# A mixer and mixture-of-experts layer on one core: row normalisation of the last mixer block on ScalarE, and four smaller moves

## What is computed

```python
xn = layernorm(x)                       # no gamma, no beta
# mixer
xi, g = split(xn @ W_in.T)              # 512 -> 2 x 1024
u  = silu(causal_conv4(xi) + conv_b)
h_t = 0.95 * h_(t-1) + 0.05 * (u_t @ W_B.T)     # 64 states, per sequence
y  = (h @ W_C.T + D_param * u) * silu(g)
mixer = layernorm(y @ W_out.T + xn) * ln_gamma + ln_beta
# experts, 8 of them; each takes its 1024 best rows
scores = (tanh(xn @ gate_w.T) + 1) / 2
vals, idx = top_k(scores.T, 1024)
r = layernorm(xn[idx]) * ffn_gamma + ffn_beta
o = (gelu(r @ fc1.T + b1) @ fc2.T + b2) * vals
out = x + mixer + scatter_add(xn, idx, o)
```

## Time and profile before

| | us |
|---|---|
| three runs | 2670.35, 2671.75, 2673.03 |
| median | 2671.75 |
| profiled execution, its own time | 2671.86 |
| its span, first to last instruction | 2670.1 |
| PE, DVE, ACT, POOL busy | 2633.7, 2057.1, 1490.4, 674.4 |
| mean granted TensorE clock | 0.998 of full |

### The profile page before, as it was taken

One profiled execution on the slowest core, in us unless ns is written; L12 is line 12 of the kernel. 1 busy time (PEld: TensorE's weight loads), 2 busy tenths in 40 slices (PEclk: granted clock), 3 DMA queues, 4 the chain that ended last, 5 costly groups with the idle time before them and its releaser, 6 DMA issues.

```text
span 2670.1 us, 41531 instructions
## 1 busy us (share of the span) xinstructions
PE 2633.7 (99%) x11818; PEld 2135.5 (80%) x11820; DVE 2057.1 (77%) x3533; ACT 1490.4 (56%) x2570; POOL 674.4 (25%) x1002
## 2 busy tenths in 40 slices
PE   8999999999999999999999999999999999999998
PEld 3588888888887788888788888888888888888886
DVE  8778888887887788888876777867778677786654
ACT  5744555555555565665445555565555655556553
POOL 5422222222222122223422213213132131321102
PEclk9999999999999999999999999999999999999999
DMA  9733222223333322235444425334253342533313
GB/s 364 259 126 111 81 92 89 91 93 104 111 111 111 110 73 87 87 93 160 142 131 109 124 64 137 90 92 133 64 136 90 91 132 65 136 90 89 99 54 71
DMA packets 139517, 299.99 MB, mean 112 GB/s; under 512 B 26080, under 2 KB 26208, under 8 KB 135520
## 3 DMA queue, kind: packets, MB, share of 16 engines
q1 hardware_dynamic: 105696, 201.54, 23.0%
q0 software_dynamic: 33664, 96.75, 14.7%
HBM read 244.46 MB, written 53.77 MB: 112 GB/s over the span
## 4 chain that ended last, share of the span: by engine, by line
PE 94%; DVE 2%; issue 1%; ACT 1%; DMA 1%; POOL 0%; SPq 0%; DVEq 0%; ACTq 0%; POOLq 0%
PE po L2485 9%; PE ring L1546 9%; PE po L2487 9%; PE po L2486 9%; PE ring L1547 8%; PE ring L1548 8%; PE pb L2485 4%; PE pb L2487 4%; PE pb L2486 4%; PE po L1584 4%; PE po L1585 4%; PE po L1586 4%; PE pc L2487 2%; PE pc L2485 2%; PE pc L2486 2%
## 5 line engine op out<-in xcount | busy, mean ns | idle before, releaser
L2485 PE MATMUL po<-w2h,hid_h 128*128 128x512 f32 x1024 | 402.2, 393 | 1.1 <-DVE hid_l L2422 1.0
L1546 PE MATMUL ring<-xt_h,w_h 128*128 128x512 f32 x1024 | 400.1, 391 | 0.1
L2486 PE MATMUL po<-w2l,hid_h 128*128 128x512 f32 x1024 | 398.6, 389 | 0.0
L1547 PE MATMUL ring<-xt_l,w_h 128*128 128x512 f32 x1024 | 398.5, 389 | 0.0
L1548 PE MATMUL ring<-xt_h,w_l 128*128 128x512 f32 x1024 | 398.4, 389 | 0.0
L1339 DVE SCALAR_TENSOR_TENSOR u<-xin,cw,u 128x512 f32<-128x512 f32 x384 | 288.4, 751 | 74.3 <-issue 32.8
L1967 POOL DMA_INDIRECT out_dram<-res,idx_c x64 | 108.6, 1697 | 476.7 <-DVE res L2332 464.7
L1546 PEld LDWEIGHTS ring<-xt_h,w_h 128*128 128x128 f32 x1024 | 192.3, 188 | 40.9 <-DVE xt_l L542 0.9
L2485 PEld LDWEIGHTS po<-w2h,hid_h 128*128 128x128 f32 x1024 | 192.3, 188 | 40.9 <-DVE hid_l L2422 1.4
L1548 PEld LDWEIGHTS ring<-xt_h,w_l 128*128 128x128 f32 x1024 | 192.2, 188 | 40.1
L1547 PEld LDWEIGHTS ring<-xt_l,w_h 128*128 128x128 f32 x1024 | 192.3, 188 | 39.3
(11 more groups left out here) (296 smaller groups left out, 6306.2 us busy)
## 6 DMA issues: line engine op xcount, KB each, us to landing
w2r<-fc_in SPq DMA_DIRECT2D x256, 256.0 KB
wo<-wo_halves POOLq DMA_DIRECT2D x120, 512.0 KB, 4.2
w1r<-fc_in SPq DMA_DIRECT2D x144, 256.0 KB
x_tail<-x_in SPq DMA_DIRECT2D x64, 256.0 KB, 2.8
out_dram<-res SPq DMA_DIRECT2D x64, 256.0 KB, 2.0
g_x<-x_in SPq DMA_DIRECT2D x15, 1024.0 KB, 8.4
xt_rows<-g_xnt SPq DMA_DIRECT2D x15, 1024.0 KB, 10.1
rows<-xt_rows SPq DMA_DIRECT2D x15, 1024.0 KB, 6.2
```

The source lines that it names most:

```text
L1546: pe.matmul(ring[r % 2][:, :], w_h[:, r, q], xt_h[:, k, :], start=(k == 0), stop=False)
L1547: pe.matmul(ring[r % 2][:, :], w_h[:, r, q], xt_l[:, k, :], start=False, stop=False)
L2485: pe.matmul(dst, ah, bh, start=start, stop=False, skip_group_check=more)
L2486: pe.matmul(dst, ah, bl, start=False, stop=False, skip_group_check=more)
```

## The change

It has five parts.

1. In the last block the first 512 rows are normalised without gamma and beta, by ACT (`normal_row`), two tiles ahead of the last gate eviction and two behind the cast of group 2. POOL adds `-mean * rstd` per tile for it. Gamma and beta come in when the transposed rows are evicted: there they are per-partition columns (`f_ln_c`, a new small load). `group_high` evicts with scale and bias into `yt_whole`, and then casts. The last `group_high` stands ahead of `first_high` and `normal_rows`. `t_low` reads `yt_whole`. DVE's `normalise` for this group is gone.
2. POOL issues `load_wo` for groups 4 and 5 ahead of and between the gate gathers.
3. In the first two one-hot blocks the fifth one-hot goes from behind group 4 to behind group 3 (`HOT_AT`); `PLACE_AT` stays.
4. The three casts of small weights in the gate stage go into the last group, one in each of its first three blocks, ahead of the wait for the scores.
5. At the start SP sets 37 semaphores ahead of the gate weights and of the second load of x. In the first expert pass the third and fourth row tile of expert 1 move from steps 13 and 14 to 12 and 13.

```diff
@@ stage_gate, sync
+        m.counts.start(sp, sums.counts)
+        m.counts.start(sp, m.counts.counts[begun:own])
         sp.dma_start(gw[:, :, :], t["gate_w"]).then_inc(c_gw, 16)
         load_x(1, 1)
-        m.counts.start(sp, sums.counts)
-        m.counts.start(sp, m.counts.counts[begun:own])
@@ stage_gate, scalar
+        def small_high(i):
+            if i == 0:
+                act.wait_ge(c_win, 48 + 1)
+                act.copy(w.wc_hh[:, :], staged2[:, 0:2, :].rearrange("p a b -> p (a b)")).then_inc(c_sh, 1)
...
         def group(h, first=False, last=False):
...
                     normalise(b + 1, (i + 1) % R)
+                if last and i < 3:
+                    small_high(i)
                 act.wait_ge(c_se, (b + 1) * KD + 1)
@@ Experts
         self.yt_end = m.ends_at["xt_l"]
+        self.yt_w = m.over("yt_whole", self.yt_end, KD * TB * 4, [P, KD, TB])
...
-    def inverse_std(self, pool, g, half):
+    def inverse_std(self, pool, g, half, with_shift=False):
...
+            if with_shift:
+                pool.wait_ge(self.c_rs, n + 1 + 1)
+                pool.tensor_scalar(self.std[:, j:j + 1], self.mv[:, j, 0:1], self.rstd[:, j:j + 1], -1.0, ALU.mult,
+                                   ALU.mult).then_inc(self.c_g, 1)
+
+    def normal_row(self, act, j):
+        act.wait_ge(self.c_g, j + 1 + 1)
+        act.activation(self.rows[:, j, :], self.rows[:, j, :], ACT.Identity, bias=self.std[:, j:j + 1],
+                       scale=self.rstd[:, j:j + 1]).then_inc(self.c_nm, 1)
@@
-HOT_AT = 2 * ((START, 0, 1, 2, 4, 5),) + 4 * ((START, 0, 1, 3, 5),)
+HOT_AT = 2 * ((START, 0, 1, 2, 3, 5),) + 4 * ((START, 0, 1, 3, 5),)
@@ stage_mixer, sync
+        sp.dma_start(ew.columns[:, :, :], t["f_ln_c"]).then_inc(ew.c_small, 16)
@@ stage_mixer, gpsimd, turn
             if last:
-                ew.inverse_std(pool, 0, ends.half)
+                ew.inverse_std(pool, 0, ends.half, True)
                 for j in range(J):
+                    if j % 2 == 0:
+                        load_wo(b, WO + j // 2)
                     ew.gather_gates(pool, 0, j)
                 ends.twice_scale(pool, b)
-            for c in range(WO, NC_):
+            for c in range(WO + 2 if last else WO, NC_):
                 load_wo(b, c)
@@ stage_mixer, scalar
         def group_high(k):
             act.wait_ge(c_t, k + 1 + 1)
-            act.copy(xt_h[:, k, :], rows_out[k % 2][:, :]).then_inc(c_th, 1)
+            if k == 0:
+                act.wait_ge(ew.c_small, 16 + 1)
+                act.wait_ge(c_ag, NB * NW + 1)
+            act.activation(ew.yt_w[:, k, :], rows_out[k % 2][:, :], ACT.Identity, bias=ew.columns[:, 1, k:k + 1],
+                           scale=ew.columns[:, 0, k:k + 1]).then_inc(c_whole, 1)
+            act.wait_ge(c_whole, k + 1 + 1)
+            act.copy(xt_h[:, k, :], ew.yt_w[:, k, :]).then_inc(c_th, 1)
...
             if last:
+                ew.normal_row(act, 0)
+                ew.normal_row(act, 1)
                 in_g(b, 7)
             y_high(b, 2)
+            if last:
+                ew.normal_row(act, 2)
+                ew.normal_row(act, 3)
...
+                if last and k == KD - 1:
+                    group_high(k)
                 if last and k >= 2:
                     sums.first_high(act, k - 2)
                 ends.normal_rows(act, b, k)
-            if last:
-                group_high(KD - 1)
@@ stage_mixer, vector
         def t_low(n, k, last=False):
             dve.wait_ge(c_th, n + 1 + 1)
-            dve.tensor_tensor(xt_l[:, k, :], rows_out[k % 2][:, :] if last else next_x[:, k * TB:(k + 1) * TB],
+            dve.tensor_tensor(xt_l[:, k, :], ew.yt_w[:, k, :] if last else next_x[:, k * TB:(k + 1) * TB],
...
         def expert_rows(c):
...
-            if 1 <= c < 1 + J:
-                ew.normalise(dve, 0, c - 1, rows)
             if c == J:
                 ew.keep(dve, 0, 0)
@@ stage_experts
-    TAIL_AT, ROWS_1_AT, ROWS_2_AT = (4, 5, 6, 7), (3, 5, 7, 8), (9, 11, 13, 14)
+    TAIL_AT, ROWS_1_AT, ROWS_2_AT = (4, 5, 6, 7), (3, 5, 7, 8), (9, 11, 12, 13)
```

More of the change, by code:

```diff
@@ L591, in normalise @@
                                scale=rstd[i % 2][:, j:j + 1]).then_inc(c_xa, 1)
+        def small_high(i):
+            if i == 0:
+                act.wait_ge(c_win, 48 + 1)
+                act.copy(w.wc_hh[:, :], staged2[:, 0:2, :].rearrange("p a b -> p (a b)")).then_inc(c_sh, 1)
+            elif i == 1:
+                act.copy(w.wc_lh[S:P, :], staged2[S:P, 0:2, :].rearrange("p a b -> p (a b)")).then_inc(c_sh, 1)
+            else:
+                act.wait_ge(c_id, 4 + 1)
+                act.copy(w.wb[:, :, 0:S], staged2[:, 3, :].rearrange("p (c s) -> p c s", s=S)).then_inc(c_sh, 1)
         def group(h, first=False, last=False):
@@ L639, in __init__ @@
         self.rstd = m.sb("f_rstd", [P, J])
+        self.columns = m.sb("f_columns", [P, 2, KD])
         self.c_w1 = [m.count(f"f_w1_{i}") for i in range(4)]
```

15 lines of the change are left out of this document (6 added, 9 removed).

## The result

The changed kernel takes **2662.45 us** (median; 2662.04 to 2663.16) against 2671.78 us for the kernel before, measured beside it. The ratio is 0.9965, with a 95% interval from 0.9955 to 0.9976: 9.3 us, or 0.35%, less. One of the seven runs of the changed kernel took 5414.03 us in a slow state and is left out of the lowest-to-highest times and of the ratio. The profiled execution of the changed kernel took 2662.32 us, its span is 2660.6 us; before it was 2671.86 and 2670.1.

The account below looks back on a forecast made before the run. PE was taken as busy for 99% of the span, so only its own waits could pay. The terms -3.9 - 1.2 - 0.7 - 1.1 + 0 made -6.9 us against 2671.86, giving 2665.0 us, range 2662.6 to 2668.3.

Parts of the forecast that it names:

- The last block, -3.9: Last mixer block: normalising off DVE starts the experts at 1305.5 against 1309.38; -3.9 us, ends 0 and -5.9.
- The estimate from the Trainium skill's formula: Last block's gate gather: 2.0 us plus bytes at 436 GB/s lands it at 1290.6; share 5 loses nothing, 0.6 more gained.
- The one-hots, -1.2: First two one-hot blocks: moving the fifth one-hot gives -0.6 us each, -1.2 in all; ends +0.8 and -1.5 each.
- The expert row work, -1.1: First expert pass: earlier row work removes PE's wait for a low half and its restart; -1.1 us, ends +0.5 and -1.1.
- The casts, -0.7: Gate stage, 13th block: moving three ACT casts removes PE's wait for normalised rows; -0.7 us, ends 0 and -0.7.
- the next floor: Gate stage: DVE's statistics, released by a load, come next and limit the gain from the casts to -0.7 us.
- The start, 0: SP's semaphore increments ahead of gate weights and second x load: no gain or loss; 0, ends -0.3 and +2.1 us.
- Rival 1: Last block: gate gathers land behind the second weight load, share 5 starts 2.2 us later; 2667.2 us, chance 0.17.
- Rival 2: One-hots, casts and row work hand each wait on; only the last block gives its 3.9; 2668.0 us, chance 0.10.
- Rival 3: Last block gives -5.3 because gates land in time and ACT's chain is shorter than drawn; 2663.6 us, chance 0.15.
- Rival 4: Last block: gate gathers trickle beside weights and row transfers, landing from 1300 on gives a slower 2673 us; chance 0.03.

Follow-up runs that it names:

- gates_first: The changed kernel with POOL's old queue order in the last block, four gate-row gathers first, then the four weight loads: 2669.1 us.
- rows_undone: The changed kernel with the row work of the first expert pass back at steps 13 and 14: 2663.1 us.
- filler pair: The changed kernel with 16 extra PE transposes behind the first scores, with the new order on SP at the start (2661.9 us) and the old one (2661.8 us).
- start_alone: The kernel before with only the new order on SP at the start: 2671.4 us, ratio 1.0001.
- the kernel before with a filler: The kernel before with 16 extra identity transposes on PE behind the first block's scores, their result overwritten unread: 2670.6 us, ratio 0.9996.
- better: The changed kernel with two of ScalarE's casts moved earlier and the copy of the kept gates one product later: 2661.2 us.
- weights_first: The changed kernel with both early weight loads ahead of the four gate gathers in POOL's queue: 2665.6 us.
- hot_undone: The changed kernel with the fifth one-hot behind group 4 again in the first two one-hot blocks: 2664.2 us.

## Why the prediction was right or wrong

The time came out 2.55 us under the forecast. Between the two profiled executions the sum was off by 2.6 us, and two terms of the gate stage make 2.3 of it: the start, put at 0 and measured at -1.63, and the casts, put at -0.7 and measured at -1.37.

**The last block, -3.9: right, measured -4.1 (-4.2 alone).** The times hold share by share. With the 4.0 us by which the block now starts earlier added back, share 3 began at 1287.4 (forecast 1287.5), share 4 at 1290.6 (1290.8), share 5 at 1294.4 (1295.0), share 7 at 1302.4 (1302.8), and the experts at 1305.3 (1305.5). The fourth gather started at 1288.4 (1288.6), the gates were there at 1291.3 (1291.8), and DVE waited 1.18 us (1.6). I took 3.2 us for a gather, and DVE's copy started 2.9 us behind the start of the fourth. PE's wait at share 5, forecast beside that at share 7, is too short to be listed. The estimate from the Trainium skill's formula for a software-queue transfer (DMA: Bandwidth & Descriptors, Anatomy of one DMA) had 1290.6 and is 0.7 us early here. That the weights would be in time was right, and gates_first shows that the part stands or falls with it.

**The one-hots, -1.2: right, measured -1.0**, with both of the waits that were forecast (0.8 and 0.6, listed as 0.62 and 0.37 us of idle time; from start to start they are 1.00 and 0.64 us, with the step itself in them, 0.23 in the first).

**The expert row work, -1.1: right**, 1.0 for the wait. The stretch changed by 1.32 between the two profiled executions and by 0.66 in rows_undone, which is its scatter.

**The casts, -0.7: mis-sized, -1.4.** The step that failed is the end of this term, "the ends are 0 and -0.7". I took the one wait of 0.66 us at 93.03 and followed it back to the casts, but not the wait of 0.57 us for the evictions of the same block just ahead of it, which PE had at 88.77 in the trace of before. Both hang on ACT's three casts; together with their restarts they are the 1.4 us. The load that I named as the next floor is one only where it is late: with 12.3 us to land (gates_first) the part gave 0.6 us, near my -0.7, with 10.8 it gave 1.4. I took the late load of one execution for a rule.

**The start, 0: right for the edit as far as the runs tell, wrong for the stretch.** The filler pair says that the order is worth nothing once PE is kept busy, and start_alone changed no median. But the stretch around it had 1.6 us in it that were no wait, 1.5 of them a clock of 0.50. The step that failed is the reading of PE's waits as all that PE loses: "0, with ends -0.3 and +2.1" has no term for the clock of the execution that the sum starts from. How much of the 9.3 us between the medians is this clock stays open, since only one execution of each kernel has a profile; the kernel before with a filler came out 1.2 us lower, within what the interval allows for no change.

**The rivals.** Rival 1 (the gates ride behind the weights) is right in that the gates land later beside them, 3.9 against 3.2 us, and wrong in its price: it had share 5 another 2.2 us later, and the gates cost 0.2 there (3.83 us behind share 4, and 3.63 in better, which does not wait for them). Rival 2 (the small parts do nothing) is refuted: they gave 3.4 us. Rival 3 came nearest in time (2663.6) and for the wrong reason; the last block gave 4.1 and not 5.3. Rival 4 (slower) did not come, and weights_first and gates_first stayed below the kernel before as well. But they show what a late transfer costs: waits of PE of 1.95 and 3.6 us made the block 3.5 and 6.4 us longer, with the clock at 0.50 behind each. The prediction had no such term.

## What to carry to other kernels

Read the granted clock beside the list of waits: behind idle time of PE of 2 to 4 us these traces have it at half speed, and the profile books that as busy. Where a wait hangs on a load, ask whether the load is as late in other executions. When following a wait back to its cause, look for every wait with the same cause, not for the longest. And where two kinds of transfer share a queue, price both orders before you trust the third.

## What the runs showed of the hardware

The clock's fall behind idle time was new to me. Behind 2.9 us of idle time of PE, 16 transposes took 3.58 us instead of 1.97. Behind 3.6 us, the matmuls of 512 columns of one share started 0.43 us apart and not 0.23, and the granted clock was at 0.50 for over 5 us. At the same place of the start, idle times of 1.3 to 2.3 us had no fall behind them in eight profiles, and those of 2.35 to 2.9 us in five had one. The same 13 profiles are separated as well by the first scores, 4.07 us and more against 3.80 and less, so these runs don't say which of the two matters.

The same program differs from run to run by more than most parts of this change are worth: 2669.4 to 2674.8 us before. Loads of 1024 KB issued between 60 and 83 us took 9.5 to 12.3 us to land over the 18 profiles. From the mixer's start to the experts it hardly differs at all: the last block took 34.67 to 34.68 us in the four profiles with its old form, and 30.3 to 30.8 in nine of the ten with the new form and the new order of the loads (31.6 in hot_undone, where the gates were late). So a part of 1 us there can be read from one trace, and in the gate stage it can't.

Where POOL's subtraction started between 16.2 and 17.1 us, beside DVE's normalising, DVE's three operations took 2.3 to 2.5 us (eight profiles); where it started at 17.6 or later, they took 1.4 us (ten). It lengthens PE's idle time ahead of the second block, and changed no median that could be told.
